# A front written image by image, joined with three phases of expert slots, in a one-core attention and mixture-of-experts kernel

## Chip, core and metric

The kernel runs on one core of one Trainium2 chip. The metric is the device time in microseconds (us). The core has four computing engines that run side by side: PE (TensorE, matrix multiplication), DVE (VectorE), ACT (ScalarE) and POOL (GpSimd). SP (SyncE) issues most DMAs. The engines wait for each other on semaphores, each of them in the order of its own instructions.

## What is computed

`x` holds 8 images of 64 channels by 256 places. An attention over the places of each image is followed by a mixture of 8 experts over all 2048 tokens, each token being sent to its two best experts. Cut to what matters, with the places of all images as tokens in the second half:

```python
xf = ln_c(x)                                   # over channels, eps 1e-6
kq = w_kq @ xf + b_kq                          # 32 rows, keys and queries alike
v = w_v @ xf + b_v
attn = softmax(kq.T @ kq)                      # 256 x 256 for each image
x = x + (w_o @ (v @ attn.T) + b_o)
t = tokens(x)                                  # 2048 x 64
n = ln_t(t)                                    # eps 1e-5
p, e = top_k(softmax(n @ router_w.T), 2)
gates = p / (sum(p) + 1e-9)
t = t + sum_k gates_k * (w2[e_k] @ (silu(w1[e_k] @ n) * (w3[e_k] @ n)))   # hidden size 682
```

## The kernel before

**Front.** The 2048 tokens are 16 tiles of 128. Four blocks (index `k`) of four tiles, two images each, go through the front. In each block DVE takes the channel statistics (`statistics`, L527 and L530), POOL makes the inverse deviation by a power of -0.5 (`inverse_deviation`, L314 and L317), DVE normalises and writes each row twice (`xn`, L536), and PE turns four tiles at once (`transpose_x`, L869). The turned values are split in a high and a low part (`x_hi` by ACT, `x_lo` by DVE, type float32r), and so are keys and queries, which are stacked over 128 partitions (`kq_left`, `kq_right`, L406 to L568). PE makes keys and queries (`key_query`), values with the output projection folded in (`value_out`, L885), scores (`similarity`, L896), and, behind the softmax of ACT (`exponentials`), turns the probabilities (`transpose_probs`, L907) and applies them (`attend`, L919). DVE divides by the row sums and adds the input (`residual`, L593), takes the second statistics and normalises (`normalise_t`, L548). Then each block is turned again (`transpose_t`, L931) and multiplied by the router matrix (`route`, L940). DVE finds the two best experts (`choose`), forms the two gates (`weigh`) and, from counts that PE makes with a triangular matrix (`rank`), the row of each token in its expert's region (`positions`).

**Dispatch.** A row of `xs` in device memory holds 64 values, the token's number and its gate (66 numbers). POOL writes 128 rows at a time with an indirect DMA (`scatter_row`, L335), 32 such DMAs in all: 16 for blocks 0 and 1 in the front, and 16 in the first six rounds of the expert loop (`X_SHARE`).

**Slots.** The experts work through 39 slots of 128 rows, taken in 20 pairs. Slots are opened in three phases, 0 to 7, 8 to 15 and 16 to 38, once 2, 3 and 4 blocks are counted (`KNOWN`). For each phase DVE works out which expert and which first row each slot has (`subtiles_of_experts`, `owners_of_slots`, `rows_of_slots`: a chain of small instructions, L661 to L702). SP reads that table into registers and loads the slot's rows (`load_rows`, L269) and its expert's weights (`load_weights`, L254, 576 KB each, a ring of 8 slots). SP waits for all scattered rows of a phase (`landed`) before it loads the phase's first rows.

**Rounds.** Round `i` handles pair `i`. DVE doubles the loaded rows (`pair_up`, L800), PE turns them (`turn_x`, L1015), makes both hidden products in three steps (`up`, L1035 and L1037, 48 instructions in all), ACT applies silu (L487), DVE multiplies (`multiply`, L816), and PE multiplies by the second matrix one round later (`down`, L1053, 24 instructions) and turns the result (`turn_y`). DVE scales it by the gate (`gate`, L824) and POOL scatters it to `ys` by token (L344). Table work of later phases stands between the `multiply` calls of rounds 0 to 4 (`tables_between`). Before the first round PE runs 48 multiplications whose result nobody reads (`WARM`, L1066), waits for the last count, and starts.

**Close.** When all results have been scattered, SP loads both results of each token in four parts (L294), DVE adds them and the residual (L856, L859), PE turns (L1090), ACT copies, and SP stores 8 pieces (L298).

## Time and profile before

| | us |
|---|---|
| median of 3 runs | 230.09 (228.75 to 232.47) |
| the profiled execution, its own time | 228.14 |
| its span, first to last instruction | 226.4 |
| PE busy in the span | 168.3 (74%) |
| DVE busy | 118.2 (52%) |
| POOL busy | 85.5 (38%) |
| ACT busy | 72.3 (32%) |

The span is what the trace shows; 1.7 us of the execution's own time lie around it. The front takes the time up to about 91 us, the rounds the time from there to about 208 us, the close the rest. A busy share is an average over these three stages, which have different limits. In the rows further down, a timeline row gives the start in us, the length in us, the engine, the line of the kernel, the operation, the tile written and those read, their sizes and a count; a square bracket at its end is the idle time of the engine ahead of it and what ended that. One fp32 multiplication of PE shows as two instructions, a transpose or a float32r multiplication as one. `SPq` is SP's queue of DMA issues.

### The profile page before, as it was taken

What the parts mean: (1) busy time and instruction counts of PE and PEld (TensorE: products, weight loads), DVE (VectorE), ACT (ScalarE), POOL (GpSimd) and SP (SyncE); (2) the same over time, 40 slices, a digit from 0 to 9 for tenths busy, and PEclk for the clock granted to TensorE, in tenths of its full rate; (3) what the DMA queues carried; (4) which work ended last, traced back from release to release, by engine and by line L of the source; (5) the groups of instructions that cost most, each with busy time, mean ns of one, the idle gap of its engine ahead of it and who ended that gap; (6) DMA issues with size and microseconds to landing.
All of it is one profiled execution on the core that took longest, in us unless ns stands there. A gap on an engine that the chain in (4) does not pass through costs nothing.

```text
span 226.4 us, 5197 instructions
## 1 busy us (share of the span) xinstructions
PE 168.3 (74%) x1776; PEld 145.6 (64%) x1776; DVE 118.2 (52%) x441; ACT 72.3 (32%) x154; POOL 85.5 (38%) x110
## 2 busy tenths in 40 slices
PE   2646798799853263989599989989999999993040
PEld 2436698698742162878488877778788888882020
DVE  2696697686579185373645433444444545550050
ACT  2237443431111020334324434333435444430010
POOL 6142520202787600365503355555533334444300
PEclk9999555555555558599959999999999999999655
DMA  5970000000002986100597638887768787100154
GB/s 133 427 305 1 0 0 3 0 0 0 22 31 56 346 284 231 24 25 21 175 291 246 224 105 264 310 285 235 233 198 285 232 257 254 75 20 17 35 172 88
DMA packets 16315, 33.48 MB, mean 148 GB/s; under 512 B 7826, under 2 KB 9010, under 8 KB 15778
## 3 DMA queue, kind: packets, MB, share of 16 engines
q1 hardware_dynamic: 14018, 30.80, 41.1%
q0 software_dynamic: 2272, 2.36, 3.1%
q8 instruction: 14, 0.23, 0.4%
q14 instruction: 11, 0.09, 0.1%
HBM read 25.94 MB, written 7.21 MB: 146 GB/s over the span
## 4 chain that ended last, share of the span: by engine, by line
PE 50%; DVE 16%; issue 15%; SPq 7%; DMA 4%; ACT 3%; POOL 2%; POOLq 1%; another core or an unknown queue 0%; DVEq 0%; ACTq 0%
PE bank L1035 21%; PE bank L1053 12%; PE bank L919 6%; PE bank L1015 2%; DVE xn L536 2%; SPq L262 2%; DVE kq_right L568 2%; SPq L254 2%; PE bank L907 2%; SPq L269 2%; DMA y_in<-ys 2%; SPq L258 1%; PE bank L869 1%; DVE parts L527 1%; DVE t_sb L593 1%
## 5 line engine op out<-in xcount | busy, mean ns | idle before, releaser
L1035 PE MATMUL bank<-x_cols,weights 64*128 64x128 f32 x468 | 66.2, 290 | 3.5 <-DVE hid L816 2.0
L1037 PE MATMUL bank<-x_cols,weights 64*128 64x128 f32 x468 | 66.2, 290 | 0.0
L1035 PEld LDWEIGHTS bank<-x_cols,weights 64*128 64x128 f32 x468 | 58.0, 196 | 10.9 <-issue 9.6
L816 DVE TENSOR_TENSOR hid<-bank,act_sb 128x512 f32<-128x512 f32 (+1 forms) x60 | 40.4, 676 | 44.8 <-ACT act_sb L487 41.5
L1037 PEld LDWEIGHTS bank<-x_cols,weights 64*128 64x128 f32 x468 | 58.0, 195 | 0.1
L344 POOL DMA_INDIRECT ys<-y_out,y_row x39 | 37.4, 960 | 47.1 <-PE bank L1035 32.7
L487 ACT ACTIVATE act_sb<-bank 128x512 f32<-128x512 f32 (+1 forms) x60 | 35.1, 586 | 57.5 <-PE bank L1035 43.6
L335 POOL DMA_INDIRECT xs<-rows,pos x32 | 31.1, 973 | 38.7 <-PE bank L1035 30.8
L1053 PE MATMUL bank<-hid,weights 128*64 128x128 f32 x468 | 34.8, 285 | 5.8 <-issue 5.4
L1053 PEld LDWEIGHTS bank<-hid,weights 128*64 128x64 f32 x468 | 28.0, 141 | 10.3 <-issue 8.1
L314 POOL TENSOR_SCALAR variance<-moments 128x4 f32<-128x4 f32 x8 | 1.9, 232 | 39.5 <-DVE moments L530 39.5
L919 PE MATMUL bank<-u_sb,probsT 128*128 128x65 f32 x64 | 14.5, 410 | 1.6 <-DVE probsT L580 1.6
L919 PEld LDWEIGHTS bank<-u_sb,probsT 128*128 128x128 f32 x64 | 13.9, 324 | 2.5 <-DVE probsT L580 2.5
L800 DVE COPY x_pairs<-x_in 128x256 f32<-128x256 f32 (+1 forms) x20 | 6.2, 310 | 14.9 <-DMA x_in<-xs 14.9
L1015 PE MATMUL bank<-ident,x_pairs 128*128 128x128 f32 x39 | 9.2, 317 | 3.6 <-DVE x_pairs L800 3.6
L480 ACT COPY x_cols<-bank 128x256 f32<-128x256 f32 (+1 forms) x20 | 7.3, 365 | 13.5 <-PE bank L1015 12.5
L1090 PE MATMUL bank<-ident,total_y 128*128 128x128 f32 x8 | 2.7, 445 | 9.6 <-DVE total_y L859 9.4
L940 PE MATMUL bank<-proj,t_cols 64*128 64x8 f32 x32 | 7.5, 360 | 2.3 <-ACT t_cols L437 2.3
L940 PEld LDWEIGHTS bank<-proj,t_cols 64*128 64x128 f32 x32 | 7.1, 325 | 3.0 <-ACT t_cols L437 2.9
L424 ACT ACTIVATE probs<-bank,neg_max 128x256 f32<-128x256 f32 x16 | 6.3, 474 | 7.6 <-DVE neg_max L573 7.6
L317 POOL TENSOR_TENSOR rstd<-variance,neg_half 128x4 f32<-128x4 f32 x8 | 8.4, 1049 | 0.7
L824 DVE TENSOR_TENSOR y_out<-bank,x_in 128x128 f32<-128x128 f32 (+1 forms) x20 | 5.6, 278 | 5.2 <-PE bank L1062 5.2
(138 smaller groups left out, 208.5 us busy)
## 6 DMA issues: line engine op xcount, KB each, us to landing
weights<-experts SPq DMA_DIRECT2D x39, 576.0 KB
xs<-zeros SPq DMA_DIRECT2D x4, 1056.0 KB, 8.8
x_in<-xs SPq DMA_DIRECT2D x39, 33.0 KB
y_in<-ys SPq DMA_DIRECT2D x4, 256.0 KB, 4.0
ys<-y_out,y_row POOLq DMA_INDIRECT x39, 3.8
xs<-rows,pos POOLq DMA_INDIRECT x32
out<-result SPq DMA_DIRECT2D x8, 64.0 KB, 2.1
x_sb<-x_tok SPq DMA_DIRECT2D x1, 384.0 KB, 3.5
```

The costliest lines, as they stand in the source:

```text
L317: nc.gpsimd.tensor_tensor(rstd[:, norm, tiles(k)], variance[:, norm, tiles(k)], neg_half[:, tiles(k)], ALU.pow).then_inc(rstd_ready, 1)
L335: nc.gpsimd.indirect_dma_start(xs, bass.IndirectOffsetOnAxis(ap=pos[:, k, at:at + 1], axis=0), rows[:, TPB * k + at // K_TOP, at % K_TOP, ...
L344: nc.gpsimd.indirect_dma_start(ys, bass.IndirectOffsetOnAxis(ap=y_row[:, j:j + 1], axis=0), y_out[:, i % RING, h, :], None).then_inc(y_sca ...
L480: nc.scalar.copy(x_cols[:, i % 2, 0:n], X_BANK[:, 0:n]).then_inc(x_cols_ready, 1)
L487: nc.scalar.activation(live(i, act_sb[:, g % 3, :]), live(i, H1_BANK[g % 2][:]), ACT.Silu).then_inc(silu_done, 1)
L816: nc.vector.tensor_tensor(live(i, hid[:, g % HRING, :]), live(i, H3_BANK[g % 3][:]), live(i, act_sb[:, g % 3, :]), ALU.mult).then_inc(hid_ ...
L919: ins = nc.tensor.matmul(O_BANK[:, at + (C + 1) * i:at + (C + 1) * (i + 1)], probsT[:, b % 2, j, P * i:P * (i + 1)], u_sb[:, 2 * b + j, :] ...
L940: ins = nc.tensor.matmul(U_BANK[:, E * t:E * (t + 1)], t_cols[:, k % 2, P * t:P * (t + 1)], proj[0:C, CK:CK + E], start=True, stop=True)
L1015: ins = nc.tensor.transpose(X_BANK[:, P * h:P * (h + 1)], x_pairs[:, i % 2, h, :, :], ident[:])
L1035: first_ = nc.tensor.matmul(H1_BANK[g % 2][:, dst], weights[0:C, slot, at:at + P], x_cols[0:C, i % 2, src], start=True, stop=True)
L1037: second_ = nc.tensor.matmul(H3_BANK[g % 3][:, dst], weights[C:P, slot, at:at + P], x_cols[C:P, i % 2, src], start=True, stop=True)
L1053: ins = nc.tensor.matmul(Y_BANK[C * h:C * (h + 1), 0:P], weights[:, slot, at:at + C], hid[:, g % HRING, src], start=(chunk == 0), stop=(ch ...
```

## The change

The front is written anew. It goes image by image (8 images of two tiles, index `b`) in plain fp32: the split in high and low parts, the doubling of `xn` and the stacking of keys and queries are gone. The router matrix is multiplied into the value matrix at the start, so that `attend` delivers 8 router scores beside the 64 channels and the row sum (73 columns where it was 65); `transpose_t` and `route` are gone, and the x part of the scores is added by DVE (`x_logits`, `residual`). The best two experts are found in scores that are not yet scaled by the deviation, which does not change their order.

`KNOWN` counts images now: 4, 6 and 8. 26 of the 32 row scatters are issued ahead of POOL's part of the rounds and 6 in rounds 0 to 2. The row has no gate any more (65 numbers). Gates are formed for all tokens at once behind the last round (`gate_shifts`, `weigh`) and applied to the loaded results, and the residual is added by PE into the same bank. The 48 idle multiplications are gone. SP issues the weights of pair 0 alone before `landed(0)`; ACT issues half of the last loads and stores. The row of code to read for the order of the stages:

```diff
-KNOWN = (2, 3, NBLK)
+KNOWN = (4, 6, B)
-WARM = 48
-X_SHARE = (3, 3, 3, 3, 2, 2)
+ROWS_AT_ONCE = TPB * K_TOP * 6 + 2
+ROWS_OF_ROUND = (2, 2, 2)
@@ SP
-            for i in pairs_of(0):
-                load_weights(i, owners_of(i))
+            load_weights(0, owners_of(0))
             early_rows = [rows_of(i) for i in range(2)]
             landed(0)
             for i in pairs_of(0):
                 load_rows(i, early_rows[i] if i < 2 else rows_of(i))
+                if i > 0:
+                    load_weights(i, owners_of(i))
@@ POOL
+            t_deviation(0)
+            rows_done, results_done = 0, 0
+            for b in range(B):
+                own = range(TPB * K_TOP * b, min(TPB * K_TOP * (b + 1), ROWS_AT_ONCE))
+                for n in own:
+                    if n == own[-1] and b + 1 < B:
+                        t_deviation(b + 1)
+                    scatter_row(n)
+                    rows_done += 1
@@ DVE
+            for b in range(B):
+                residual(b)
+                if b == B - 2:
+                    pair_up(0)
+                choose(b)
+                if b + 2 < B:
+                    row_max(b + 2)
+                t_statistics(b)
+                carry_on(b)
+                if b + 3 < B:
+                    x_logits(b + 3)
+                positions(b)
+                normalise_t(b)
+                if b + 1 == KNOWN[0]:
+                    subtiles_of_experts(0)
+                    owners_of_slots(0)
+                    rows_of_slots(0)
+            pair_up(1)
+            used_up(0)
+            subtiles_of_experts(1)
...
-                if (i, s) == (0, 0):
-                    used_up(1)
-                elif (i, s) == (0, 1):
-                    subtiles_of_experts(2)
-                elif (i, s) == (1, 1):
+                if (i, s) == (0, 0):
+                    owners_of_slots(1)
+                elif (i, s) == (0, 1):
+                    rows_of_slots(1)
+                elif (i, s) == (1, 1):
+                    used_up(1)
+                elif (i, s) == (1, 2):
+                    subtiles_of_experts(2)
+                elif (i, s) == (2, 1):
                     owners_of_slots(2)
-                elif (i, s) == (2, 1):
+                elif (i, s) == (3, 1):
                     rows_of_slots(2)
@@ PE
+            for b in range(B - 1):
+                attend(b)
+                if b + 3 < B:
+                    transpose_x(b + 3)
+                if b + 2 < B:
+                    similarity(b + 2)
+                if b + 3 < B:
+                    key_query(b + 3)
+                    value_out(b + 3)
+                if b + 1 < B:
+                    transpose_probs(b + 1)
+                rank(b)
...
-            pe.wait_ge(t_ready, TPB * NBLK)
-            for _ in range(WARM):
-                nc.tensor.matmul(O_BANK[:, 0:P], ones[:], before[:], start=True, stop=True)
             turn_x(0)
-            pe.wait_ge(rank_read, NBLK)
-            pe.wait_ge(counts_ready, PHASES)
+            attend(B - 1)
             for i in range(NT + 2):
                 if i < NT:
                     up(STEPS * i)
+                    if i == 0:
+                        rank(B - 1)
+                        pe.wait_ge(t_ready, B)
                     up(STEPS * i + 1)
```

The probabilities' transposes have one bank (`PT_BANK`) where they had two, and `attend` has one half-bank that `residual` has to read before the next `attend`.

On PE, the last block's share of the front and the start of the rounds before (L907, L919: attention; L931, L940: turning and routing; L952 to L962: `rank`; L1066: the idle multiplications; L1015: `turn_x`):

```order
L907 MATMUL bank<-ident,probs 128x128 x8
L919 MATMUL bank<-u_sb,probsT 128x65 x8
L931 MATMUL bank<-ident,rows 64x128 x4
...
L940 MATMUL bank<-proj,t_cols 128x8 x4
L931 MATMUL bank<-ident,rows 64x128 x4
...
L940 MATMUL bank<-proj,t_cols 128x8 x4
L952 MATMUL bank<-taken,before 128x32
...
L1066 MATMUL bank<-before,ones 128x128 x48
L1015 MATMUL bank<-ident,x_pairs 128x128 x2
```

On PE, one full image and the start of the rounds now (lines of the changed kernel: L899 `attend`, L856 `transpose_x`, L878 `similarity`, L863 `key_query`, L869 `value_out`, L888 `transpose_probs`, L911 to L918 `rank`, L962 `turn_x`, L982 `up`):

```order
L899 MATMUL bank<-u_sb,probsT 128x73 x4
L856 MATMUL bank<-ident,xn 64x128 x2
L878 MATMUL bank<-kq 128x256 x2
L863 MATMUL bank<-xT,proj 32x256
L869 MATMUL bank<-wu_x,xT 128x81 x2
L888 MATMUL bank<-ident,probs 128x128 x4
L911 MATMUL bank<-taken,before 128x16
...
L962 MATMUL bank<-ident,x_pairs 128x128 x2
L899 MATMUL bank<-u_sb,probsT 128x73 x4
L982 MATMUL bank<-x_cols,weights 128x128
```

The first pair's rows are turned ahead of the last image's `attend`, and its first products stand ahead of the last `rank`.

On POOL, the second deviations and the row scatters before:

```order
L314 TENSOR_SCALAR variance<-moments 128x4
L317 TENSOR_TENSOR rstd<-variance,neg_half 128x4
L335 DMA xs<-rows,pos 16384x66 x8
L314 TENSOR_SCALAR variance<-moments 128x4
L317 TENSOR_TENSOR rstd<-variance,neg_half 128x4
L335 DMA xs<-rows,pos 16384x66 x24
```

And now (L330, L333: `t_deviation`; L343: `scatter_row`), of which the last three pieces:

```order
L343 DMA xs<-xrows,pos 16384x65 x4
L330 TENSOR_SCALAR variance_t<-moments_t 128x2
L333 TENSOR_TENSOR rstd_t<-variance_t,neg_half 128x2
L343 DMA xs<-xrows,pos 16384x65 x2
L330 TENSOR_SCALAR variance_t<-moments_t 128x2
L333 TENSOR_TENSOR rstd_t<-variance_t,neg_half 128x2
L343 DMA xs<-xrows,pos 16384x65 x7
```

A deviation now stands ahead of the last scatter of each image, so that DVE's `normalise_t` of image `b + 1` waits for three scatters of image `b`.

## Rows read from the trace of the kernel before

**Rows 1.** The page, slices: the clock granted to PE, one digit per 5.66 us.

```profile
PEclk9999555555555558599959999999999999999655
```

**Rows 2.** Windows: us, then busy (instructions) of PE, PEld, DVE, ACT, POOL, clock, DMA.

```profile
45.00:55.00 10.00, 9.46 (x47) 8.89 (x48) 7.04 (x40) 2.85 (x7) 0.11 (x1) 0.50 0.00 0
```

**Rows 3.** Timeline of PE in the front and the first rounds: start us, length us.

```profile
23.48 1.55 PE L919 MATMUL bank<-u_sb,probsT 128*128 128x65 f32 x8
...
45.99 1.97 PE L907 MATMUL bank<-ident,probs 128*128 128x128 f32 x8
47.61 1.20 PE L896 MATMUL bank<-kq_right,kq_left 128*128 128x256 f32 x4
48.77 3.68 PE L919 MATMUL bank<-u_sb,probsT 128*128 128x65 f32 x16
...
81.73 4.48 PE L1066 MATMUL bank<-before,ones 128*128 128x128 bf16 x48
...
91.67 0.42 PE L1035 MATMUL bank<-x_cols,weights 64*128 64x128 f32 x1
...
91.88 0.42 PE L1035 MATMUL bank<-x_cols,weights 64*128 64x128 f32 x1
...
99.46 0.44 PE L1015 MATMUL bank<-ident,x_pairs 128*128 128x128 f32 x2
```

**Rows 4.** Timeline of ACT, one copy of turned probabilities.

```profile
47.99 0.59 ACT L431 COPY probsT<-bank 128x512 f32<-128x512 f32 x1 [3.86 <-PE bank L907]
```

**Rows 5.** Timeline of POOL: a deviation between scatters, and the last scatter.

```profile
66.82 0.25 POOL L314 TENSOR_SCALAR variance<-moments 128x4 f32<-128x4 f32 x1
67.16 1.12 POOL L317 TENSOR_TENSOR rstd<-variance,neg_half 128x4 f32<-128x4 f32 x1
68.47 1.10 POOL L335 DMA_INDIRECT xs<-rows,pos  x1 [0.20 <-issue]
...
121.61 0.96 POOL L335 DMA_INDIRECT xs<-rows,pos  x1 [0.30 <-issue]
```

**Rows 6.** Timeline of DVE: the tables, and the first rounds.

```profile
67.09 0.28 DVE L661 SCALAR_TENSOR_TENSOR over<-taken_by,steps_sub 128x128 f32<-128x128 f32 x1
...
69.77 0.17 DVE L691 SCALAR_TENSOR_TENSOR table<-owner,row_at 128x8 int32<-128x8 f32 x1
...
83.11 0.16 DVE L706 TENSOR_SCALAR given<-ends 128x8 f32<-128x8 f32 x1
...
85.08 0.17 DVE L675 TENSOR_SCALAR given<-ends 128x8 f32<-128x8 f32 x1
...
86.55 0.17 DVE L694 SCALAR_TENSOR_TENSOR begin<-used,base 128x8 f32<-128x8 f32 x1
...
93.82 0.69 DVE L816 TENSOR_TENSOR hid<-bank,act_sb 128x512 f32<-128x512 f32 x1 [3.66 <-ACT act_sb L487]
...
109.62 0.52 DVE L800 COPY x_pairs<-x_in 128x256 f32<-128x256 f32 x1 [4.72 <-DMA x_in<-xs]
```

**Rows 7.** Timeline of SP (its DMA issues), from pair 7 to the end.

```profile
124.19 0.89 SPq L254 DMA_DIRECT2D weights<-experts  x2
131.18 0.86 SPq L269 DMA_DIRECT2D x_in<-xs  x2
...
213.47 1.76 SPq L294 DMA_DIRECT2D y_in<-ys  x4
219.20 5.28 SPq L298 DMA_DIRECT2D out<-result  x8
```

**Rows 8.** The chain that ended last, in order of time: four pieces of PE.

```profile
115.87 2.76 PE bank L1053 x24
...
167.18 0.37 PE bank L1015 x2
...
173.77 1.46 PE bank L1053 x24
...
192.26 0.37 PE bank L1015 x2
```

More of the change, by code:

```diff
@@ L6 @@
 F32 = mybir.dt.float32
-F32R = mybir.dt.float32r
 BF16 = mybir.dt.bfloat16
@@ new lines, in key_query, with value_out @@
+            def key_query(b):
+                pe.wait_ge(xT_ready, b + 1)
+                if b >= 1:
+                    pe.wait_ge(kq_ready, b)
+                nc.tensor.matmul(K_BANK[0:CK, 0:N], wk, xT[0:C, b % 2, :], start=True, stop=True).then_inc(kq_done, 1)
+            def value_out(b):
+                if b >= 1:
+                    pe.wait_ge(u_ready, b)
+                for i in range(TPB):
+                    ins = nc.tensor.matmul(U_BANK[:, UX * i:UX * (i + 1)], xT[:, b % 2, P * i:P * (i + 1)], wu_x[:],
+                                           start=True, stop=True)
```

896 lines of the change are left out of this document (405 added, 491 removed).

## Prediction, made before the changed kernel was run

> **What bounds the kernel now.** I read the clock in slices first, then one window of the front, the timelines of PE, POOL, DVE and SP around the start of the rounds, and last the chain of waits. The granted clock is at half, 1.2 GHz, from the fifth slice, about 25 us, up to the rounds, apart from one slice at 85 us, and full, 2.4 GHz, in nearly all of the rounds [rows 1]. The first `attend` starts at 23.5 us [rows 3]. In a window in the middle of the front PE is busy 9.5 of 10 us, DVE 7.0 and POOL 0.1 [rows 2]: the front is bound by PE at 1.2 GHz, and POOL, which must issue the row scatters, stands idle. Its last deviation lies between scatters at 66.8 [rows 5]; phase 0 has its table at 69.9, phase 1's chain runs from 83.1 to about 88, and the first `multiply` comes only at 93.8 [rows 6]. So from the end of attention, about 62, to 94 PE has little to do: the stretch is set by POOL's 16 scatters, DVE's small chains and loads. In the rounds I use the turning of pair i's rows as a marker. Pair 2 is turned at 99.46 [rows 3], pair 13 at 167.18, pair 18 at 192.26 [rows 8]. The last five rounds take 5.02 us each and are pure PE; the eleven before them take 6.16 each, 12.5 us more than at 5.02. Two places explain most of it: DVE idles 4.7 us for the rows of pair 4 up to 109.6 [rows 6], since SP waits for phase 1's rows, which POOL issues between rounds; and SP's load for pair 8 goes out at 131.2, 7 us behind the weights of pair 7 [rows 7], since the last scatter of phase 2 goes out at 121.6 [rows 5]. Each leaves a cold or a starved PE behind.
>
> **The front, image by image.** PE's work per image at 1.2 GHz, in order. `attend`: 8 instructions; 16 take 3.7 us [rows 3], so 1.8. `transpose_x` and `transpose_probs`: 6 transposes; 8 take 1.6 (45.99 to 47.61) [rows 3], so 1.2. `similarity` is fp32 now: an instruction over 128 columns takes 0.21 (91.67 to 91.88) [rows 3], over 256 columns 0.43, four of them 1.7, against 1.2 for two images before [rows 3]; `key_query` two, 0.85. `value_out` is 4 instructions of 81 columns, at `attend`'s 0.23 each 0.9. `rank` 0.2. Sum 6.7. With one bank for the turned probabilities the next `attend` also waits for ACT's copy, 0.6 [rows 4] plus handing over, 0.8 in all: 7.5 us an image. The window before shows half of a block's DVE work at 3.5 us [rows 2]; with twice the number of small instructions I take 4.8, which fits. The start: the chain to the first `attend` loses the stacking but takes fp32 scores; I walk it to 20.6, between 18 and the 23.5 of before.
>
> So `attend(b)` starts at 20.6, 28.1, 35.6, 43.1, 50.6. Behind image 3 DVE makes phase 0's table, 67.1 to 69.9, 2.9 us [rows 6], with hand-overs 3.3; the second statistics of image 4 come at 57.9.
>
> **POOL takes over.** A scatter costs 0.96 and a gap of 0.30, 1.26 together; a deviation between two scatters 1.35 (66.82 to 68.47 less one gap) [rows 5]. An image is 4 × 1.26 + 1.35 = 6.4 us: under the 7.5 at first, but behind the table POOL is late and then works without a pause. From 57.9 up to the end of `t_deviation(7)` there are 10 scatters (one of image 3, four each of 4 and 5, one of 6) and 4 deviations: 12.6 + 5.4, with waits 76.4. PE is through attention at about 68 and waits. DVE then has `normalise_t(7)`, `pair_up(1)` and the chain that before ran from 83.1 to 85.1 [rows 6]: 0.6 + 0.5 + 2.0, first `multiply` at 79.5, where it was 93.8. Before it all phase 0 rows have landed: their last scatter goes out at about 60, and pair 0's rows can be there by 65.
>
> **Round 0 and 1.** `owners_of_slots(1)` and `rows_of_slots(1)`, 1.5 and about 1.4 (85.08 to 86.55 and on) [rows 6], are now between the first three `multiply`, so `multiply` 1 is at 82.3 and `up` of round 1 goes slowly. Pair 2 is turned at 85.0: 14.5 us earlier than at 99.5.
>
> **The rounds.** The wait for pair 4 goes: rows of images 4 and 5 are out at about 73, phase 1's table at 84. The one for pair 8 goes too: the last six scatters leave in rounds 0 to 2. What is late next is the weights' ring (a slot is free when `down` is through) and PE itself. Sixteen rounds at 5.02 are 80.3; I add 2.2 for a half clock up to round 2. That makes pair 18 at 167.5, against 192.3. Of the 24.8 us, 14.5 are from the front and 10.3 from the rounds.
>
> **The idle multiplications.** They ran from 81.7 for 4.5 us [rows 3]; the clock rose in that slice but was at half in the next, when the first products ran at 0.21 an instruction [rows 1, 3]. I cost their removal at nothing, at most 2 us. The Trainium skill's page "TensorE: Matmul & The Clock Gate" (section "Part 1: The HAM clock gate") speaks against the removal: the default is half rate and only sustained activity releases it. The trace agrees with that for both levels, but shows that this warm-up was spent before the work came.
>
> **The close.** From pair 18's turn to the end are 34.1 us. The gate work moves behind the last round, where DVE waits for the scatters anyway; ACT's table load and one exponential lie there too. Per quarter DVE's first instruction is twice as wide, 0.2 to 0.3 more, 1.0 in all; the eight stores take SP 5.3 us to issue [rows 7] and are split over two queues, which saves about 1.5. Net -0.5, between -2 and +2.
>
> The loads of x go to SBUF in pieces of 256 bytes; no row has this, the nearest is that rows of 264 bytes are read in each round without holding up the last five. Bounds 0 to +2; I take 0. The Trainium skill's page "DMA: Bandwidth & Descriptors" (section "Specifications") wants pieces of at least 512 bytes for the line rate. By it the load of images 2 to 7 would take up to twice as long, an estimate, which is within those bounds.
>
> **Sum.** 167.5 + 34.1 - 0.5 = 201.1 us of span, with the 1.7 around it 202.8. The profiled execution of before, 228.1, is 2.0 below its median of 230.1; by the median the sum would be 204.8. I take 203.5.
>
> **Rivals.** (1) The front is faster: the clock is full for longer, as it is in the first slices [rows 1], or DVE's chain is shorter. PE then takes less than 6.4 per image and POOL sets everything: from its first row scatter at 27 to `t_deviation(7)` 25 scatters and 7 deviations, 31.5 + 9.5, give 68 to 70 instead of 76.4, and 196. Against it: PE is at 1.2 GHz in the same stage before, and as busy. (2) The rounds keep their 6.16: the waits named are gone but the weights, 1.15 MB per round, come late, or more small steps hold the loop. 16 × 1.14 = 18 us instead of 2.2: 219. For it: eleven rounds of sixteen are like that; against it: each long wait has a cause that the change takes away. (3) The front is slower: engines wait for each other across one bank more than 0.8, 1.5 us more in each of 6 images, 9 us: 212. For it: every hand-over is exposed twice as often. (4) The other side, slower than before: without the idle multiplications and with a PE that waits from 68 to 80 and between the first `multiply`, the clock stays at half through the rounds. A `down` then takes 2.76 against 1.46 us [rows 8], the 48 instructions of `up`, two side by side, 24 × 0.21 = 5.1 us, so a round takes 8 to 8.8 instead of 5.02, 3.8 more. It is slower than before from 8 such rounds, by over 2% from 9; all twenty would give 277. Against it: before, the loop also began at half clock and left it within two slices [rows 1], and back-to-back work is what it gets from round 2.
>
> **How the numbers follow.** My forecast, 203.5, has 0.60 (its own range 198 to 209), rival 1 0.15, rival 2 0.12, rival 3 0.09, rival 4 0.04. The range that leaves out some 2 in 10 goes from 194 to 215. A measurement of this kernel can tell about 2% from no change, 4.6 us. Rivals 1 to 3 are all faster by more, up to mixtures of 2 and 3, which reach 228: 0.93 faster, 0.03 within, 0.04 slower.
>
> **What would show it.** Right: first `attend` at 19 to 22; half clock and 7.5 us between `attend` of images 1 to 4; POOL without a pause from about 58 to 76; first `multiply` at 78 to 81; pair 2 turned at 85; no wait of DVE for `x_in`; 5.0 us between turned pairs from pair 4 on; 34 us from pair 18 to the end. Wrong: a full clock in the front (rival 1), weights or rows that PE or DVE wait for in the rounds (2), PE idle in attention by more than 1 us an image (3), half clock past round 3 (4).

## The result, and the profile after

| | kernel before | changed kernel |
|---|---|---|
| median | 229.42 us (227.37 to 232.47, 4 runs) | 203.27 us (202.06 to 205.86, 4 runs) |
| profiled execution, its own time | 228.14 us | 205.86 us |
| its span | 226.4 us | 204.1 us |

The ratio is 0.887, with a 95% interval of 0.877 to 0.897: 11% faster, 0.2 us from the 203.5 forecast. The profiled execution of the changed kernel happens to be the longest of its four, so the walk below adds up to 204.1, not to 201.5, the span that goes with the median.

The walk has two markers, the turning of the rows of pair 2 and of pair 18 (`turn_x`, which turns a pair's rows one round ahead of its products). Timeline of PE in the changed kernel; start us, length us, line (L899 is `attend`, L878 `similarity`, L863 `key_query`, L962 `turn_x`, L1000 `down`):

```profile
21.45 1.90 PE L899 MATMUL bank<-u_sb,probsT 128*128 128x73 f32 x8
23.14 0.63 PE L856 MATMUL bank<-ident,xn 128*64 128x128 f32 x2
23.70 2.07 PE L878 MATMUL bank<-kq 32*128 32x256 f32 x4
25.70 1.06 PE L863 MATMUL bank<-xT,proj 64*32 64x256 f32 x2
26.69 1.14 PE L869 MATMUL bank<-wu_x,xT 65*128 65x81 f32 x4
27.63 1.06 PE L888 MATMUL bank<-ident,probs 128*128 128x128 f32 x4
...
29.36 1.98 PE L899 MATMUL bank<-u_sb,probsT 128*128 128x73 f32 x8 [0.61 <-ACT probsT L446]
...
61.36 1.98 PE L899 MATMUL bank<-u_sb,probsT 128*128 128x73 f32 x8 [0.61 <-ACT probsT L446]
...
93.33 0.44 PE L962 MATMUL bank<-ident,x_pairs 128*128 128x128 f32 x2
94.90 1.53 PE L1000 MATMUL bank<-hid,weights 128*64 128x128 f32 x24
...
98.34 0.44 PE L962 MATMUL bank<-ident,x_pairs 128*128 128x128 f32 x2
...
168.62 0.44 PE L962 MATMUL bank<-ident,x_pairs 128*128 128x128 f32 x2
```

The first `attend` stands at 21.45 (23.48 in [rows 3]), and from 29.36 to 61.36 lie four images, 8.00 us each. Pair 2 is turned at 86.28 (99.46 in [rows 3]), pair 3 at 93.33, and from pair 4, at 98.34, every round takes 5.02 us up to pair 18 at 168.62 (192.26 in [rows 8]). So pair 2 comes 13.2 us earlier, the sixteen rounds take 82.3 us instead of 92.8, and from pair 18 to the end it is 35.5 instead of 34.1: 13.2 + 10.5 - 1.4 = 22.3, which is 226.4 less 204.1.

Windows of the changed kernel, the stage that [rows 2] shows of before (us, then busy (instructions) of PE, PEld, DVE, ACT, POOL, clock, DMA share, GB/s):

```profile
40.00:50.00 10.00, 9.39 (x32) 6.23 (x32) 5.41 (x33) 3.27 (x9) 6.57 (x8) 1.00 0.07 21
```

PE is as busy as before (9.39 of 10 us), but POOL now works 6.57 us in it, where it had 0.11. Timelines of POOL and DVE at the end of the front, which answer to [rows 5, 6]:

```profile
59.53 0.24 POOL L330 TENSOR_SCALAR variance_t<-moments_t 128x2 f32<-128x2 f32 x1 [1.41 <-DVE moments_t L603]
...
72.90 0.24 POOL L330 TENSOR_SCALAR variance_t<-moments_t 128x2 f32<-128x2 f32 x1
73.22 0.72 POOL L333 TENSOR_TENSOR rstd_t<-variance_t,neg_half 128x2 f32<-128x2 f32 x1
74.14 1.12 POOL L343 DMA_INDIRECT xs<-xrows,pos  x1 [0.20 <-issue]
75.56 0.96 POOL L343 DMA_INDIRECT xs<-xrows,pos  x1 [0.30 <-issue]
76.93 0.24 POOL L330 TENSOR_SCALAR variance_t<-moments_t 128x2 f32<-128x2 f32 x1 [0.41 <-issue]
77.26 0.72 POOL L333 TENSOR_TENSOR rstd_t<-variance_t,neg_half 128x2 f32<-128x2 f32 x1
```

```profile
73.97 0.60 DVE L611 TENSOR_SCALAR xrows<-rows,moments_t,rstd_t 128x128 f32<-128x128 f32 x2 [1.79 <-POOL rstd_t L333]
...
78.01 0.60 DVE L611 TENSOR_SCALAR xrows<-rows,moments_t,rstd_t 128x128 f32<-128x128 f32 x2 [0.46 <-POOL rstd_t L333]
...
80.86 0.69 DVE L798 TENSOR_TENSOR hid<-bank,act_sb 128x512 f32<-128x512 f32 x1
```

Between 59.5 and 78 POOL has 10 scatters and 4 deviations nearly without a pause; the last deviation ends at 77.98 (76.4 forecast), and the first `multiply` starts at 80.86 (79.5 forecast, 93.82 in [rows 6]). DVE's wait of 4.72 us for the rows of pair 4 [rows 6] is gone.

One thing at the end was not in the walk. Windows of the changed kernel in which the last pair is computed, and the rows of ACT and PE in them:

```profile
180.00:182.00 2.00, 0.09 (x2) 0.00 (x0) 0.00 (x0) 0.00 (x0) 1.26 (x2) 1.00 0.08 24
182.00:184.00 2.00, 0.94 (x5) 0.97 (x6) 0.00 (x0) 0.27 (x1) 0.66 (x1) 0.78 0.08 27
184.00:186.00 2.00, 2.00 (x10) 1.59 (x8) 0.00 (x0) 0.15 (x1) 0.00 (x0) 0.50 0.00 0
```

```profile
182.65 0.27 ACT L501 COPY y_cols<-bank 128x128 f32<-128x128 f32 x1 [3.61 <-remote]
```

```profile
183.06 1.26 PE L1000 MATMUL bank<-hid,weights 128*64 128x128 f32 x5 [2.97 <-ACT y_cols L501]
```

For more than 2 us PE, DVE and ACT all stand still, with nothing that they would wait for, while POOL scatters; ACT's wait is put down to "remote", the profile's word for a releaser that it finds on no engine or queue of this core. Behind it the granted clock is at 0.50, and the last `down` (12 instructions here) runs at half pace: it takes 2.75 us, and 1.50 in a run further down without such a wait. I call this a stand-still. The kernel before has one at the same place, ahead of its last `down`:

```profile
206.27 1.49 PE L1053 MATMUL bank<-hid,weights 128*64 128x128 f32 x12 [2.61 <-issue]
```

It has others too, and the experiments had to tell what they cost.

### The profile page after: what moved, and what is told of

Its sections match the earlier page's. It is cut to its first block, busy times and chain, and to the rows that moved or that the text cites. A ratio compares the mean times of both kernels' runs of the same rounds, so it can differ in the third digit from the quotient of the medians.

```text
span 204.1 us, 5200 instructions
## 1 busy us (share of the span) xinstructions
PE 174.5 (85%) x1744; PEld 141.7 (69%) x1744; DVE 106.8 (52%) x434; ACT 75.3 (37%) x172; POOL 85.5 (42%) x119
## 4 chain that ended last, share of the span: by engine, by line
PE 68%; POOL 8%; issue 8%; DVE 6%; DMA 4%; ACT 2%; POOLq 1%; SPq 1%; ACTq 0%; DVEq 0%
PE bank L982 26%; PE bank L1000 13%; PE bank L878 6%; POOL xs L343 4%; PE bank L899 4%; PE bank L869 4%; PE bank L863 3%; PE bank L962 3%; PE bank L888 2%; DMA y_in<-ys 2%; PE bank L1045 2%; POOL ys L352 2%; PE bank L984 2%; POOL rstd_t L333 1%; PE bank L856 1%
## 5 line engine op out<-in xcount | busy, mean ns | idle before, releaser
L982 PE MATMUL bank<-x_cols,weights 64*128 64x128 f32 x468 | 67.4, 293 | 1.9 <-DVE hid L798 1.9
L982 PEld LDWEIGHTS bank<-x_cols,weights 64*128 64x128 f32 x468 | 59.0, 198 | 9.1 <-issue 7.2
L343 POOL DMA_INDIRECT xs<-xrows,pos x32 | 31.9, 998 | 22.0 <-issue 10.1
L1000 PE MATMUL bank<-hid,weights 128*64 128x128 f32 x468 | 32.9, 286 | 3.0 <-ACT y_cols L501 3.0
L1000 PEld LDWEIGHTS bank<-hid,weights 128*64 128x64 f32 x468 | 27.9, 143 | 5.6 <-issue 3.4
L899 PE MATMUL bank<-u_sb,probsT 128*128 128x73 f32 x64 | 15.6, 423 | 3.5 <-ACT probsT L446 3.5
L899 PEld LDWEIGHTS bank<-u_sb,probsT 128*128 128x128 f32 x64 | 14.3, 329 | 4.1 <-ACT probsT L446 4.1
L878 PE MATMUL bank<-kq 32*128 32x256 f32 x32 | 16.6, 670 | 0.0
L878 PEld LDWEIGHTS bank<-kq 32*128 32x128 f32 x32 | 9.3, 319 | 4.1 <-issue 1.9
L869 PEld LDWEIGHTS bank<-wu_x,xT 65*128 65x128 f32 x32 | 7.4, 321 | 6.0 <-issue 5.7
L962 PE MATMUL bank<-ident,x_pairs 128*128 128x128 f32 x39 | 9.4, 323 | 0.1
L564 DVE TENSOR_REDUCE neg_max<-bank 128x2 f32<-128x512 f32 x8 | 5.5, 691 | 7.4 <-PE bank L878 7.2
L1045 PEld LDWEIGHTS bank<-ident,total_y 128*128 128x128 f32 x16 | 3.3, 292 | 8.7 <-DVE total_y L846 8.3
L869 PE MATMUL bank<-wu_x,xT 65*128 65x81 f32 x32 | 9.1, 438 | 0.3 <-DVE wu_x L742 0.3
L863 PE MATMUL bank<-xT,proj 64*32 64x256 f32 x16 | 8.5, 631 | 1.0 <-ACT xT L421 1.0
L501 ACT COPY y_cols<-bank 128x128 f32<-128x128 f32 (+1 forms) x20 | 5.3, 263 | 10.8 <-PE bank L1000 6.9
```

Of the source, the lines that this page charges most:

```text
L343: nc.gpsimd.indirect_dma_start(xs, bass.IndirectOffsetOnAxis(ap=pos[:, b, at:at + 1], axis=0), xrows[:, TPB * b + at // K_TOP, at % K_TOP, ...
L863: nc.tensor.matmul(K_BANK[0:CK, 0:N], wk, xT[0:C, b % 2, :], start=True, stop=True).then_inc(kq_done, 1)
L869: ins = nc.tensor.matmul(U_BANK[:, UX * i:UX * (i + 1)], xT[:, b % 2, P * i:P * (i + 1)], wu_x[:], start=True, stop=True)
L878: ins = nc.tensor.matmul(S_BANK[b % 2][:, N * i:N * (i + 1)], kq[:, b % 3, P * i:P * (i + 1)], kq[:, b % 3, :], start=True, stop=True)
L899: ins = nc.tensor.matmul(O_BANK[:, (TX + 1) * i:(TX + 1) * (i + 1)], probsT[:, b % 2, j, P * i:P * (i + 1)], u_sb[:, 2 * b + j, 0:TX + 1], ...
L962: ins = nc.tensor.transpose(X_BANK[:, P * h:P * (h + 1)], x_pairs[:, i % 2, h, :, :], ident[:])
```

## The experiments

The runs fell on three chips, one for each set, on which the kernel before takes different times: 215.3 us (13 runs), 228.8 us (7 runs) and 216.8 us (7 runs). I call the one of the second set slow and the others quick; the first measurement, with 229.4, is like the slow one. The changed kernel as it is was measured on no quick chip; the nearest is the burst run of the third set. Ratios are to the kernel before on the same chip; single kernels are compared only within a set, or by their profiles.

### First set, a quick chip: four edits

**The idle multiplications, taken from the kernel before.**

```diff
-WARM = 48
+WARM = 0
```

> The kernel before without its 48 idle multiplications (WARM = 0). My theory: they bought nothing, since in the kernel before they ended at 86.2 us, PE then waited 3.6 us for the first rows, and the first products ran at 0.21 us an instruction; the time stays within 1 us, first products at half rate for about 4 us as before. Rival, that the idle work shortens the slow stretch at the start of the rounds: 2 to 4 us slower.

Measured: 216.19 us, ratio 0.999 (0.995 to 1.004). Their removal is free on this chip, as forecast; the slow one did not run it. The run has a second use: its span is 215.2 us, 11.2 less than the 226.4 of the profile before, for the same work. Where those 11 us lie is read below. They are the chip's: the kernel before itself takes 215.3 here.

**Phase 1's rows sent earlier in the kernel before.**

```diff
-X_SHARE = (3, 3, 3, 3, 2, 2)
+X_SHARE = (6, 6, 4)
```

> The kernel before, with its 16 late row scatters in rounds 0 to 2 as 6, 6 and 4 instead of 3, 3, 3, 3, 2 and 2 in rounds 0 to 5. My theory: the late scatters caused both long waits of the rounds (rows of pair 4, load for pair 8). Pair 2's turn stays at 99.5 us, from there to pair 18's turn 92.8 us become 83 to 85, the whole 8 to 9 us faster. Rival, that the weights' transfers or the loop itself held eleven rounds at 6.2 us: at most 3 us faster.

Measured: 212.82 us, ratio 0.990 (0.982 to 0.998), 2.5 us less by the medians, where 8 to 9 were expected; that is within the 2% that counts as no change. By the profiles, from pair 2 to pair 18 it takes 84.9 us, against 88.8 in the run without idle multiplications. The direction is right and the size is not: 3.9 us, where I had expected 8 to 9, because on this chip the rounds had only 8.4 us above 5.02 each to lose, and DVE still waits 3.73 us for rows at 102.6. That 84.9 is within the 83 to 85 that I gave for the rounds says little, since this chip starts from 88.8 and not from 92.8.

**Rows sent late in the changed kernel.** The other direction: 16 scatters in the front, the rest as before.

```diff
-ROWS_AT_ONCE = TPB * K_TOP * 6 + 2
-ROWS_OF_ROUND = (2, 2, 2)
+ROWS_AT_ONCE = TPB * K_TOP * 4
+ROWS_OF_ROUND = (3, 3, 3, 3, 2, 2)
...
+                if not own and b + 1 < B:
+                    t_deviation(b + 1)
```

> The changed kernel with the old share of scatters: 16 in the front (images 0 to 3), then 3, 3, 3, 3, 2 and 2 in rounds 0 to 5; the deviations of images 5 to 7 have no scatter ahead of them. My theory: the front gets only 1 to 2 us shorter, because attention ends where it did (PE, then DVE), and the rounds get their two waits back, pair 2 to pair 18 89 to 93 us instead of 82.3; in all 5 to 9 us slower than the changed kernel, 208 to 212. Rival, that POOL's queue is what sets the end of the front: first multiply 5 us or more earlier (75 instead of 80.9), and the whole within 3 us of the changed kernel.

Measured: 206.53 us, ratio 0.963 (0.955 to 0.971). The first `multiply` comes at 79.96 instead of 80.86, and pair 2 to pair 18 takes 87.5 us, below the 89 to 93 expected; DVE waits for rows again, timeline of DVE in this run:

```profile
95.90 0.29 DVE L763 COPY x_pairs<-x_in 128x256 f32<-128x256 f32 x1 [5.26 <-DMA x_in<-xs]
102.48 0.29 DVE L763 COPY x_pairs<-x_in 128x256 f32<-128x256 f32 x1 [2.26 <-DMA x_in<-xs]
```

The 206.5 is a little under the 208 to 212 expected. So the ten scatters cost the front only 0.9 us, although POOL works them off without a pause: without them PE's attention and DVE's chains end nearly as late.

**The similarity in one part.** Each fp32 product stands in the profile as two instructions; with the operand typed as `F32R` (float32r) it is one. The run leaves out the low part of keys and queries, so its scores are less exact; it is there to price the instructions.

```diff
-        kq = sb("kq", [CK, 3, N])
+        kq = sb("kq", [CK, 3, N], F32R)
```

> The changed kernel with keys and queries rounded to float32r; their low part is left out. The scores of an image then take 2 instructions of about 0.27 us instead of 4 of 0.50. My theory, PE bound in the front: an image takes 6.5 us instead of 8.0 up to where POOL's 6.3 us an image binds, first multiply at 71 to 73 instead of 80.9, the whole 8 to 10 us faster. Rival, that hand-overs between engines set the image's time: 4 us faster or less.

Measured: 191.61 us, ratio 0.892 (0.885 to 0.899). The `similarity` of an image takes 0.72 us instead of 2.00, and an image 6.72 us (25.37 to 45.53 are three) instead of 8.00, the first `multiply` comes at 72.25, and DVE's wait for POOL grows, as it does if PE had been the limit and POOL is next:

```profile
65.15 0.60 DVE L612 TENSOR_SCALAR xrows<-rows,moments_t,rstd_t 128x128 f32<-128x128 f32 x2 [2.60 <-POOL rstd_t L334]
```

1.28 us less of PE's work made the image 1.28 us shorter, and bought 8.6 us at the first `multiply`: the front is bound by PE nearly up to its end, and POOL takes over only in the last images.

### Second set, the slow chip: the changed kernel and three versions

**The changed kernel as it is.**

> The changed kernel as it is, beside the kernel before on the chip on which the experiments run, where the kernel before takes 215.3 us instead of 229.4. If what the change takes away is work and waits of its own (image period 8.0 us, first multiply at 80.9, turn of pair 2 at 86.4, 82.3 us from pair 2 to pair 18), this kernel repeats its profile and ends at 202 to 204 us here too, 12 us faster than the kernel before. If the chip as a whole is faster, it ends near 191. With it the run with the late rows (206.5 us) should stand 3 to 5 us slower, by its 87.5 us from pair 2 to pair 18.

Measured: 203.53 us (201.88 to 206.36), ratio 0.889 (0.882 to 0.896); the profile is that of the first one, turn for turn (pair 2 at 86.23, pair 3 at 93.27). The expectation set this chip equal to the first set's, which it is not: the run was to show the changed kernel where the kernel before takes 215.3, and it stood beside 228.8. It repeats the first measurement, with 25.2 us gained, and does not decide between the two cases. The nearest run on a quick chip took 200.4, close to the first case (202 to 204) and not to 191.

**Tables moved one image forward.**

```diff
+                if b == KNOWN[1]:
+                    used_up(0)
+                    subtiles_of_experts(1)
             pair_up(1)
-            used_up(0)
-            subtiles_of_experts(1)
```

> The changed kernel with the counts of phase 0's slots and the first part of phase 1's table moved from behind image 7's rows to behind image 6's, where VectorE waits 1.8 us for GpSimd's deviation. My theory: the 2.0 us of tables between 78.8 and 80.8 stand between the last rows and the first multiply, so the first multiply comes at about 79.0, TensorE's waits of 0.48 and 1.40 us at 81.7 and 84.3 go, and the whole is 1 to 2.5 us faster. Rival: TensorE's eight-by-two up instructions at the half rate (each group 1.8 us) bound the first rounds by themselves, and the time stays within 0.7 us; or GpSimd's scatters end the front, and the first multiply stays at 80.9.

Measured: 203.30 us, the same. I had put the tables behind image 6's normalised rows, and the wait that was to hide them stands ahead of these, so they delayed image 7 by what they no longer cost at the end: the first `multiply` is at 80.83. The placing was wrong, so the theory is not tested here; the profile still shows one thing. PE has no wait around 84 us; its `up` instructions lie 0.21 us apart up to 83.8 and 0.11 from 84.0, and from then on it stays at full pace:

```profile
80.00:90.00 10.00, 9.89 (x126) 8.69 (x126) 8.44 (x32) 4.24 (x9) 5.08 (x7) 1.00 0.38 127
```

In the changed kernel the same window has 8.09 us of PE, 78 matmuls and a clock of 0.70 (run of this set). Pair 3 is turned at 90.53 instead of 93.27, 2.7 us earlier, and all later turns with it. That is what the half clock behind the two short waits at 81.7 and 84.3 costs in the profiled execution. The medians are equal, so not every execution pays it.

**20 scatters in the front, 4 in each of the first three rounds** (with the moved tables).

```diff
-ROWS_AT_ONCE = TPB * K_TOP * 6 + 2
-ROWS_OF_ROUND = (2, 2, 2)
+ROWS_AT_ONCE = TPB * K_TOP * 5
+ROWS_OF_ROUND = (4, 4, 4)
...
+                if not own and b + 1 < B:
+                    t_deviation(b + 1)
```

> As the run with the moved tables, and with 20 scatters in the front and 4 in each of the first three rounds, instead of 26 and 2. GpSimd then has 6 scatters (7.5 us) fewer in the front, so no wait of VectorE for a deviation over 0.7 us; the first multiply at 78 to 78.5. The rows of phase 1 are on their way behind pair 0 and those of phase 2 behind pair 2, 12 us ahead of pair 8, so no wait of VectorE for the rows of pair 4 or 8 over 1 us. Together 2.5 to 3.5 us faster than the changed kernel. Rival: the rows of pair 4 come late as with 16 scatters (there 5.3 us of wait), and what the front gains the rounds give back: 0 or 1 to 3 us slower.

Measured: 208.35 us, ratio 0.911 (0.905 to 0.917): 4.8 us slower than the changed kernel, where 2.5 to 3.5 faster was expected and 3 slower at most. Neither case foresaw how. DVE waits for no rows; the first `multiply` is at 79.55; the time goes to stand-stills. Timelines of PE and ACT in this run:

```profile
86.49 1.72 PE L1003 MATMUL bank<-hid,weights 128*64 128x128 f32 x21
88.61 0.27 PE L1003 MATMUL bank<-hid,weights 128*64 128x128 f32 x1 [0.40 <-issue]
89.33 0.31 PE L1003 MATMUL bank<-hid,weights 128*64 128x128 f32 x1 [0.45 <-issue]
90.04 0.27 PE L1003 MATMUL bank<-hid,weights 128*64 128x128 f32 x1 [0.40 <-issue]
```

```profile
90.81 0.60 ACT L495 ACTIVATE act_sb<-bank 128x512 f32<-128x512 f32 x1 [4.08 <-remote]
```

Windows of this run, a microsecond each:

```profile
88.00:89.00 1.00, 0.48 (x3) 0.07 (x2) 0.00 (x0) 0.00 (x0) 0.69 (x2) 1.00 0.16 31
89.00:90.00 1.00, 0.31 (x1) 0.19 (x2) 0.00 (x0) 0.00 (x0) 0.73 (x1) 1.00 0.10 33
```

Twenty-one instructions of `down` take 1.72 us (undisturbed, all 24 take 1.53), the last three come 0.72 us apart, with a granted clock of 1.00; then, from 91 us, it is at 0.50. DVE and ACT do nothing meanwhile. It is the same in the next round, 97.0 to 98.8. POOL sends four scatters in a row in both, from 85.0 and from 93.1.

**The same with the similarity in one part.**

> As the run before it in this list (20 scatters in the front, moved tables), and with the similarity's operand kept as one part, so that each similarity is 2 instructions instead of 4; the low part of keys and queries is left out. The run with that alone took 191.6 us, first multiply at 72.25, bound by GpSimd at the end of the front (VectorE waited 2.6 us for a deviation). Without GpSimd's 7.5 us there the first multiply should come at 68 to 70, and the whole at 187.5 to 189.5. Rival: the front is bound by TensorE again (6.7 us an image, last attention at about 64.5) and the first multiply stays above 71: 190.5 or more.

Measured: 198.17 us, ratio 0.866 (0.860 to 0.872). The first `multiply` comes at 70.23, 10.6 us ahead of the changed kernel's and close to the 68 to 70 expected, and pair 2 is turned in time, at 75.35. Then two stand-stills in `down` as above (79.3 and 87.1 us) put pair 3 at 83.48 and pair 4 at 90.92, where the run with the same front and no bursts, further down, has 80.24 and 85.26. The whole is 8.7 us above the upper end of the 187.5 to 189.5 expected.

### Third set, a quick chip: are the bursts to blame?

With this question open I looked for stand-stills in the profile of before. Timeline of PE there; the six rounds up to the turn of pair 13 take 5.9 to 6.3 us instead of 5.02 (130.93 to 167.11), and in each the last instructions of `down` come late, as in this one, and ACT has a wait of 1.9 to 2.8 us put down to "remote":

```profile
130.93 0.44 PE L1015 MATMUL bank<-ident,x_pairs 128*128 128x128 f32 x2
...
134.61 0.38 PE L1053 MATMUL bank<-hid,weights 128*64 128x128 f32 x2 [0.59 <-issue]
...
136.90 0.44 PE L1015 MATMUL bank<-ident,x_pairs 128*128 128x128 f32 x2
...
167.11 0.44 PE L1015 MATMUL bank<-ident,x_pairs 128*128 128x128 f32 x2
```

In these rounds POOL sends three scatters in a row (130.4, 131.6, 132.9), in all later ones two. In the front there is a long stand-still. `route` of the last block starts at 72.88 and takes 1.87 us; DVE's next instruction that needs it starts 5 us later; its wait lies across the last of a run of eight scatters (68.47 to 78.41):

```profile
72.88 1.87 PE L940 MATMUL bank<-proj,t_cols 64*128 64x8 f32 x8
```

```profile
79.81 0.32 DVE L604 MAX8 sorted<-bank 128x8 f32<-128x8 f32 x3 [5.50 <-remote]
```

On the quick chip (run without idle multiplications) the same instruction follows `route` at once:

```profile
72.87 0.24 DVE L604 MAX8 sorted<-bank 128x8 f32<-128x8 f32 x2 [0.48 <-PE bank L940]
```

How much of the 5 us reached the rounds is another question. On the quick chips DVE has its tables earlier and then waits for the first rows (timeline of DVE in the run with rows sent earlier; 4.50 us in the one without idle multiplications):

```profile
84.78 0.29 DVE L800 COPY x_pairs<-x_in 128x256 f32<-128x256 f32 x1 [4.78 <-DMA x_in<-xs]
```

Those rows lie behind eight weights, with which the DMA engines are over 90% busy from 72 to 82 us. Without idle multiplications the first pair is turned at 85.83, and at 89.80 on the slow chip, 4.0 us apart, and 1.9 of these 4.0 are there before the wait begins (the last block's `transpose_t` starts at 69.09 and 71.02). So the wait of 5.5 us can have cost some 2, not 5.

**Bursts in the changed kernel.**

```diff
-                for n in range(0 if paced else HALVES + i % 2):
+                for n in range(0 if paced else 2 * HALVES * (i % 2)):
```

> The changed kernel with GpSimd's result scatters in bursts: four in each odd round from round 3 on and none in the even ones, instead of two in nearly every round. The number of scatters is the same. Behind it is something that the profiles show and that I had not seen in my prediction: in the kernel before, the six rounds from 130.9 to 167.1 us take 5.9 to 6.3 us instead of 5.02, and in each of them GpSimd sends three scatters in a row and TensorE's down stands still for 0.3 to 1.0 us with nothing that it waits for; with 20 rows in the front and four scatters in a row in rounds 1 and 2 the same stand-still was 2.5 and 1.5 us. Theory: a third and fourth scatter in a row hold TensorE up; the rounds with four take 6.5 to 8 us, and the whole is 10 us or more slower than the changed kernel. Rival: the stand-still has to do with the rows' destination or the time of the first rounds; every round stays at 5.02 and the time stays within 1 us (the last scatters of the close may shift by one, 1.3 us). On a chip like that of the first experiments, where three in a row cost nearly nothing, the first case would be weaker: 0 to 5 us.

Measured: 200.36 us, ratio 0.927 (0.920 to 0.934). It did not test what it was to test: POOL's third and fourth scatter of a round wait for `y_out` of the next pair, so its profile has pairs of scatters with at least 1.3 us of idle time behind each (165.80, 167.06, 169.35, 170.61) and no burst. Every round from pair 3 takes 5.02 us. What is left is nearly the changed kernel on a quick chip: first `multiply` at 80.86 as there, pair 2 at 85.35, pair 18 at 165.88, span 198.1. Its last pair has no stand-still, though POOL sends seven scatters in a row around it:

```profile
177.80 1.50 PE L1000 MATMUL bank<-hid,weights 128*64 128x128 f32 x12 [0.46 <-ACT y_cols L501]
```

**Twenty in the front, two a round.**

```diff
-ROWS_AT_ONCE = TPB * K_TOP * 6 + 2
-ROWS_OF_ROUND = (2, 2, 2)
+ROWS_AT_ONCE = TPB * K_TOP * 5
+ROWS_OF_ROUND = (2, 2, 2, 2, 2, 2)
...
+                if not own and b + 1 < B:
+                    t_deviation(b + 1)
```

> The changed kernel with 20 scatters in the front and two in each of the first six rounds: never more than two in a row in the rounds. The theory of bursts expects no stand-still of TensorE without a releaser, unlike the run with 20 and 4, 4, 4 (2.5 and 1.5 us there). The first multiply at 79.5. Instead VectorE waits for the rows of pair 4 (24 rows are out only in round 1) 2 to 4 us, and for pair 8's (the last rows in round 5) 1 to 4 us, and the results run behind, so that later rounds have three scatters: 205 to 212 us in all. Rival: the stand-still stays though no burst is there.

Measured: 202.16 us, ratio 0.935 (0.929 to 0.942), 1.8 us above the run before it. The wait for pair 4 did not come (pair 4 is turned at 95.71, a 5.02 round); those around pair 8 did: DVE waits 2.63 and 3.43 us at 113.9 and 119.7, and two rounds take 5.4 and 5.8. Later rounds have three scatters in a row, every other one, and take 5.02 on this chip. The 205 to 212 expected was too high. As a test of bursts it is empty, since no profile from a quick chip has a wait put down to "remote".

**The similarity in one part, the tables where they belong.** Now ahead of image 6's rows.

```diff
-        kq = sb("kq", [CK, 3, N])
+        kq = sb("kq", [CK, 3, N], F32R)
...
+                if b == KNOWN[1]:
+                    used_up(0)
+                    subtiles_of_experts(1)
                 normalise_t(b)
...
-            used_up(0)
-            subtiles_of_experts(1)
```

> Similarity in one part (two instructions instead of four; the low part of keys and queries is left out), 26 and 2, 2, 2 scatters as in the changed kernel, and the tables (used-up slots of phase 0, first part of phase 1's) moved ahead of the wait for image 6's deviation, where VectorE idled 2.6 us. No bursts, so against the run with 20 rows in the front (198.2) the rounds come back to 5.02: 188.5 to 191.5 us. Rival: on this chip the simplified similarity alone gives less than on the first (191.6), for a reason in the chip: 194 or more.

Measured: 188.86 us, ratio 0.873 (0.867 to 0.880), as expected, and the fastest of all. DVE's wait of 2.60 us is down to 0.74, and the first `multiply` is at 70.09 (72.25 without the move, on the other quick chip).

**The late rows again.**

> The changed kernel with 16 scatters in the front and 3, 3, 3, 3, 2, 2 in the rounds, as before, again, on the chip of this set. On the first chip it took 206.5 us, waits for rows of 5.3 and 2.3 us, and its rounds with three scatters 5.03 us. If this set's chip is one where bursts cost (the kernel before at 229), the eight rounds with three scatters take about 6 us and the time is 212 to 216; if it is one where they don't (the kernel before at 215), 206 to 207 again. Rival: the chips differ in something else, and this kernel stands at 206 to 208 on either.

Measured: 208.04 us, ratio 0.963 (0.954 to 0.971), the same ratio as on the first quick chip, and in microseconds a little above the 206 to 207 expected for one. Against the burst run of the same set it is 7.7 us slower: pair 2 is turned 0.8 earlier (84.54 against 85.35), and from there to pair 18 it takes 8.4 longer (88.97 against 80.53).

### What the stand-stills are worth

The walk from the two kernels' profiles, on either kind of chip:

| | before | changed | gain |
|---|---|---|---|
| slow chip: pair 2 turned | 99.46 | 86.28 | 13.2 |
| pair 2 to 18 | 92.8 | 82.3 | 10.5 |
| pair 18 to end | 34.1 | 35.5 | -1.4 |
| quick chips: pair 2 turned | 94.22 | 85.35 | 8.9 |
| pair 2 to 18 | 88.8 | 80.5 | 8.2 |
| pair 18 to end | 32.2 | 32.2 | 0.0 |

(Quick chips: the kernel before without idle multiplications, and the changed one with the result scatters moved by a round, from two chips.) The profiles gain 22.3 us on the slow chip and 17.1 on the quick ones. From quick to slow, the kernel before takes 11.2 us longer (5.2, 4.0 and 1.9 by the three rows) and the changed one 6.0 (0.9, 1.8 and 3.3). By the medians the two kinds lie further apart, 26.2 and 25.2 us gained on the slow chips and 16.4 on the quick one, since the changed kernel's profiles there (204.1 and 204.6 us) lie above the span of its median, 201.5. So 16 to 17 us of the gain are the change's own, and 5 to 9 are the slow chip's, which takes more from the kernel before.

Not all of that is stand-stills. In the kernel before the six rounds up to pair 13 lie 6.1 us above 5.02 each; the quick chip's price for the late pair 8, two rounds of 5.44 and 5.59 us and 1.0 together, bounds what is not a stand-still in them. At the end 2.2 us are one (2.61 of idle time ahead of the last `down`, 0.46 on quick chips), and in the front some 2 may be. In the changed kernel 2.5 us at the end are one; the half clock behind it and the one in round 2 make up most of the rest.

What a stand-still is stays open. In the profiles of the slow chips each of more than 1 us lies in or right behind a run of at least three scatters; quick chips have the same runs without it. But such a run is not enough on a slow chip either: the kernel before has four runs of three row scatters in its first rounds (from 93.4, 98.1, 103.8 and 109.1), and its `down` beside the second and the third of them takes its full-pace 1.53 us, as here:

```profile
100.92 1.53 PE L1053 MATMUL bank<-hid,weights 128*64 128x128 f32 x24
```

The one at the last `down` is in all six profiles from chips of the slow kind (2.6 to 3.0 us of idle time ahead of it) and in none of the eight of quick chips (0.46). No run made bursts alone on the slow chip: the one that was to do so formed none, and fell on a quick chip. The Trainium skill's page "NOTIFIC — the notification-queue block" (section "7.1 Overflow: three behaviours, one of which stalls the engine") describes, as one of three settings, that engines are held up by their own event records when those are not drained; no run here shows whether that is at work. Nor does any view here tell whether the engines stood for want of instructions, which the profile shows arriving by two queues of their own (25 packets) without a time.

## Why the prediction was right

**The front.** The mechanism held: PE at half pace is the limit, and POOL takes over at its end. Taking 1.28 us of `similarity` out of an image shortened the image by 1.28 us and the front by 8.6; taking ten scatters out shortened it by 0.9. The terms: `attend` at 21.45 for 20.6. The image takes 8.00 us for 7.5, and the term that was mis-sized most is `similarity`, scaled from `up`'s 0.21 a 128 columns to 0.43: it takes 0.50 (23.70 to 25.70 for four), and so does each of `key_query`, together 0.45 us. The six transposes take 1.4 for 1.2 (0.56 from 23.14, 0.85 from 27.63). The hand-over at `probsT`, 0.8, is 0.6. Against this POOL's deviation was overrated: 0.24 + 0.72 us for two tiles, where I had taken the 0.25 + 1.12 for four [rows 5]. The two errors partly cancel: the first `multiply` is at 80.86 for 79.5, and pair 2 is turned at 86.28 for 85.0. Rivals 1 and 3 fall with it: 196 needed a faster PE, 212 an image of 9 us.

**The rounds.** 82.3 us from pair 2 to 18, forecast 82.5: sixteen at 5.02 and 2 us for a half clock in the first, both seen in the profiled execution (pair 2 to 3 takes 7.05, and 5.3 in the burst run on a quick chip, whose granted clock stays at 1.00). Rival 2 falls: each round from pair 4 takes 5.02. Rival 4 falls: the half clock ends with round 2.

The step that was wrong, although the number came out, is where before's 12.5 us went: "Two places explain most of it". The wait for pair 4 does explain 6.5 of them, up to pair 5 at 120.90. The late load of pair 8 [rows 7] does not explain the six rounds behind it: on a quick chip it is as late and costs 1.0 us. The other 5 are stand-stills, which I had averaged into "6.16 each" without looking at one of the rounds. That the change removes them is partly luck: its results have no backlog, so POOL sends no three in a row in the rounds. The load itself was also misread: 121.61 in [rows 5] is not the last row scatter; two more follow, and the load at 131.18 comes 4.6 us behind the start of the last:

```profile
126.62 0.96 POOL L335 DMA_INDIRECT xs<-rows,pos  x1 [0.30 <-issue]
```

In the same way the 14.5 us of the front were to come from scatters, chains and loads. On the quick chips the front brings 8.9; 4.3 of the 13.2 on the slow one are there only because the kernel before is slower on that chip, some 2 of them perhaps by the wait marked "remote", which [rows 6] stepped over. So the forecast gain of 26.6 us is met by 26 on the slow kind of chip and by 16 on the quick one, though the time there, 200.4 for nearly the same kernel, is near the forecast too: that the gain came out is luck in that much.

**The idle multiplications** cost and gave nothing, shown by themselves on a quick chip: ratio 0.999. The Trainium skill's page "TensorE: Matmul & The Clock Gate" (section "Part 1: The HAM clock gate") says that the throttled state is the default and that activity releases it, which speaks for a warm-up; here one that ended 5 us before the first product (86.2 and 91.1 us) changed nothing.

**The close.** Forecast -0.5, measured +1.4, and 0.0 on quick chips. The gates hide as planned: from the last turned result to the end it takes 17.4 us, before 17.9 (18.1 in both on quick chips). What I missed lies ahead of that. It is not so much the stand-still at 180 us, 2.97 us of idle time against 2.61 in the kernel before, as the half clock behind it: the last `down` takes 2.75 us and took 1.49.

**Not separated.** No run takes apart the rest of the change: the router folded into the values, the order of SP's first loads (the rows of pair 0 no longer lie behind eight weights), the single bank for the turned probabilities, the gates at the end. Of the front's gain, what each gives is not shown.

## What to carry to other kernels

A mean over rounds that differ hides two causes under one name: print the turn of every round, and open one of the rounds that are slow without a long wait. Rows that later rounds read belong in the front as long as the engine that sends them is not what ends it: ten scatters there cost 0.9 us and bought 8.4 in the rounds. When a rate is scaled from another instruction, take one with the same number of columns; here 128 to 256 was off by 17%, six times an image. Compare the two kernels on more than one chip before you call a gain the change's own.

## What the runs showed of the hardware

**The granted clock recorded ahead of its first fall says nothing.** The slices of the changed kernel read

```profile
PEclk9999999999999999759999999999999999997958
```

full throughout the front; it is first recorded below 1.00 behind 84 us. But the pace in the front is half. Timeline of PE in the changed kernel, `up` at 77 us and at 91 us:

```profile
77.06 0.42 PE L982 MATMUL bank<-x_cols,weights 64*128 64x128 f32 x1
...
77.27 0.42 PE L982 MATMUL bank<-x_cols,weights 64*128 64x128 f32 x1
...
91.67 0.27 PE L982 MATMUL bank<-x_cols,weights 64*128 64x128 f32 x1
...
91.78 0.27 PE L982 MATMUL bank<-x_cols,weights 64*128 64x128 f32 x1
```

They lie 0.21 us apart in the front and 0.11 in the rounds, and in the kernel before, 0.21 goes with a recorded 0.50 [rows 1, 3]. So PE ran the front, 94% busy from 40 to 50 us, at 1.2 GHz. The mean granted clock of this run, 0.957, overstates it. The first four digits in [rows 1] are as little a measure: they hide both levels. Timeline of PE in the kernel before, `value_out` of the first and of the second block:

```profile
10.30 0.40 PE L885 MATMUL bank<-wu,x_hi 128*128 128x64 f32 x1
10.51 0.40 PE L885 MATMUL bank<-wu,x_lo 128*128 128x64 f32 x1
...
20.42 0.28 PE L885 MATMUL bank<-wu,x_hi 128*128 128x64 f32 x1
20.53 0.28 PE L885 MATMUL bank<-wu,x_lo 128*128 128x64 f32 x1
```

**Chips differ by more than most changes.** The kernel before takes 215, 217, 229 and 229 us. The changed one takes 203 on the slow kind; nearly the same kernel takes 200 on a quick one, so the ratio is 0.89 on the one kind and 0.93 on the other.

**Pieces of 256 bytes** cost little: the 384 KB of images 2 to 7 took 3.9 us against 3.5, inside the bounds of 0 to 2 and far from the "up to twice as long" of the prediction's estimate.
